# Two cross-attentions of a fused two-layer Perceiver: context loads per batch element, and LayerNorm, copy and output-projection work placed elsewhere

## What is computed

```python
x = x + cross_attention_0(layernorm(x), ctx)   # Wq, Wk, Wv, Wo with biases, 16 heads of 16
x = x + self_attention_0(layernorm(x))
x = x + mixture_of_experts(layernorm(x))       # 8 experts, the best 2 of each token
x = x + cross_attention_1(layernorm(x), ctx)   # one Wq makes q, k and v; Wo; no biases
x = x + causal_rotary_attention_1(layernorm(x))
x = x + ternary_linear(layernorm(x))

def cross_attention(q, ctx):                   # softmax(q k^T / 4) v, then Wo
    ...
```

## Time and profile before

| | |
|---|---|
| median of 3 runs | 2614.49 us |
| the profiled execution: its time, its span | 2609.5 us, 2607.7 us |
| PE, PEld busy | 2407.5 us (92%), 1985.3 us |
| DVE busy | 1836.6 us (70%) |
| ACT busy | 1226.1 us (47%) |
| POOL busy | 838.5 us (32%) |
| moved by DMA | 298.94 MB |
| mean granted TensorE clock | 0.964 |
| x0: first and last scores | 32.8 and 722.9 us |
| x1: first and last scores | 1395.8 and 1971.4 us |

### The profile page before, as it was taken

One profiled execution on the slowest core, in us unless ns is written; L12 is line 12 of the kernel. 1 busy time (PEld: TensorE's weight loads), 2 busy tenths in 40 slices (PEclk: granted clock), 3 DMA queues, 4 the chain that ended last, 5 costly groups with the idle time before them and its releaser, 6 DMA issues. The chain is left out here.

```text
span 2607.7 us, 102881 instructions
## 1 busy us (share of the span) xinstructions
PE 2407.5 (92%) x44640; PEld 1985.3 (76%) x44640; DVE 1836.6 (70%) x3908; ACT 1226.1 (47%) x2728; POOL 838.5 (32%) x732
## 2 busy tenths in 40 slices
PE   7999999999988858999996999998987999999997
PEld 6888888888855546888874777777776888888885
DVE  5777777777766673222226889888986788888886
ACT  4666666666544433332325666666663232332332
POOL 3333333332221112333435344443222233233231
PEclk9999999999998958999998999999998999999998
DMA  6455555554313162111107767778763000000000
GB/s 197 146 152 158 153 155 156 157 157 121 93 53 125 52 239 104 52 48 48 50 30 231 233 192 223 216 224 230 200 195 107 2 3 2 11 11 11 11 11 26
DMA packets 171903, 298.94 MB, mean 115 GB/s; under 512 B 26296, under 2 KB 104252, under 8 KB 161984
## 3 DMA queue, kind: packets, MB, share of 16 engines
q1 hardware_dynamic: 164640, 275.57, 34.9%
q0 software_dynamic: 6816, 16.79, 2.0%
HBM read 170.75 MB, written 78.77 MB: 96 GB/s over the span
## 5 line engine op out<-in xcount | busy, mean ns | idle before, releaser
L801 ACT ACTIVATE prob_x<-ps_score_x,neg_max_x 128x257 f32<-128x257 f32 x1024 | 402.5, 479 | 259.2 <-DVE neg_max_x L853 258.7
L853 DVE TENSOR_REDUCE neg_max_x<-ps_score_x 128x2 f32<-128x514 f32 x512 | 328.8, 683 | 91.7 <-PE ps_score_x L687 91.4
L698 PEld LDWEIGHTS ps_v_x<-v_wide_x,probT_x 128*32 128x32 f32 x18432 | 289.8, 109 | 134.3 <-issue 128.2
L698 PE MATMUL ps_v_x<-v_wide_x,probT_x 128*32 128x68 f32 x18432 | 337.2, 224 | 30.9 <-issue 25.8
L877 DVE STREAM_TRANSPOSE probT_x<-prob_x 128x1152 f32<-128x1152 f32 x256 | 343.9, 1344 | 0.0
L1015 POOL TENSOR_TENSOR ctxT_x_lo<-ready,ctxT_x_hi 128x514 fp32r<-128x514 f32 x128 | 153.2, 1197 | 388.8 <-ACT ctxT_x_hi L780 388.8
L2371 POOL TENSOR_TENSOR rot_s<-turned_s,swapped_s 128x512 f32<-128x512 f32 x128 | 164.4, 1296 | 326.6 <-DVE swapped_s L2300 287.3
L1015 POOL TENSOR_TENSOR split<-loaded,split 128x514 fp32r<-128x514 f32 x128 | 153.0, 1195 | 324.5 <-ACT split L780 324.5
L230 PE MATMUL ps_x<-split,w_q_x_hi 128*128 128x258 f32 x1024 | 209.2, 302 | 22.1 <-POOL split L1015 17.7
L687 PE MATMUL ps_score_x<-kT_x,q_x 32*64 32x257 f32 x4096 | 178.3, 402 | 23.6 <-ACT prob_x L801 18.6
L1911 DVE TENSOR_TENSOR hid_moe<-ps_up_moe,silu_moe 128x512 f32<-128x512 f32 x71 | 49.1, 692 | 203.3 <-PE ps_up_moe L230 203.3
(11 more groups left out here) (290 smaller groups left out, 5997.7 us busy)
## 6 DMA issues: line engine op xcount, KB each, us to landing
v_wide_x<-v_x SPq DMA_DIRECT2D x512, 76.5 KB, 2.3
v_out_x<-v_x SPq DMA_DIRECT2D x128, 306.0 KB, 3.5
v_wide_x<-v_out_x SPq DMA_DIRECT2D x512, 76.5 KB, 2.7
ready<-ctx SPq DMA_DIRECT2D x32, 1028.0 KB, 6.0
loaded<-ctx SPq DMA_DIRECT2D x32, 1028.0 KB, 6.6
gate_whole<-moe_experts SPq DMA_DIRECT2D x32, 256.0 KB, 3.2
lo_out<-gate_whole SPq DMA_DIRECT2D x32, 256.0 KB
w_moe<-lo_out SPq DMA_DIRECT2D x8, 1024.0 KB, 8.8
```

The lines of the kernel that those rows point to most:

```text
L698: ins = pe.do.matmul(self.ps_v[r * T:(r + 1) * T, b % 2, :, :], self.probT[b % 3][:, r, n * T:(n + 1) * T], self.v_wide[b % 4][:, :, r, n, ...
L801: act.do.activation(self.prob[b % 3][:, r, 0:S], self.ps[:, r, 0:S], ACT.Exp, bias=self.neg_max[b % 2][:, r:r + 1]).then_inc(*s.exp.at(tag ...
L853: dve.do.tensor_reduce(self.neg_max[b % 2][:, r], self.ps[:, r, 0:S], AX_X, ALU.max, negate=True).then_inc(*s.neg_max.at(tag, b, half))
```

## The change

In both cross-attentions:

- The context is loaded per batch element, 257 KB at a time, one load in every turn, from a DRAM array and into an SBUF buffer in which each element is contiguous. Four semaphores (one for each place in a group) replace two. A load of element `i + 7` stands in turn `i`, behind waits for the split of element `i - 1` and for the landing of element `i + 3`.

In x1 alone (`self.opening`):

- `take_stats` of the next group stands in turn 12 of the group before (turn 4 for group 1), `root` in 13 (5); scaling is two pieces of two row blocks in turns 6 and 7 on ACT (`scale_on_act`), with one more POOL multiplication (`shift`) and one more DVE one (`minus_mean`).
- `keep_attn` is on ACT, in front of the exponentials.
- `project_out` stands behind `weigh_v` and in front of `project_k`; `add_out` at the end of the same turn on DVE, no longer at the beginning of the next.
- `load_y` issues its three loads in turns 3, 4 and 5.
- The first statistics of `s1` stand in turn 4 of the last group.

In x0 alone: statistics a turn sooner (4 and 5), root in 5, scaling in 6. `bq` and `m_zero` become events of other semaphores.

```diff
-        on_act = [t for t in tags if t in ("s0", "moe")]
+        on_act = [t for t in tags if t in ("s0", "moe", "x1")]
...
-        self.pad, self.bq = count("pad", cross()), count("bq", [()])
-        self.ctx_in = [count(f"ctx_in{i}", cross(g[i::2]), 16) for i in range(2)]
+        self.pad = count("pad", [("x0",), ("bq",), ("x1",)])
+        self.ctx_in = [count(f"ctx_in{i}", cross(b[i::BPG]), 16) for i in range(BPG)]
...
-    def scale_on_act(self, act, i):
+    def scale_on_act(self, act, i, some=range(GPS)):
         c, tag = self.c, self.tag
         act.wait_ge(c.shift, tag, i)
         if i >= len(self.xn):
             act.wait_ge(c.T, tag, i - len(self.xn), KD - 1)
-        for j in range(GPS):
+        for j in some:
             ins = act.do.activation(self.rows(i)[:, j, :], self.X[:, GPS * i + j, :], ACT.Identity, bias=self.shift[:, j:j + 1],
                                     scale=self.rstd[:, j:j + 1])
-        ins.then_inc(*c.xn.at(tag, i))
+        if some[-1] == GPS - 1:
+            ins.then_inc(*c.xn.at(tag, i))
...
-        self.ctx_in = [loaded[:, i * ctx:(i + 1) * ctx].rearrange("p (k b s) -> p k b s", k=KD, b=BPG) for i in range(2)]
+        self.ctx_in = [loaded[:, i * ctx:(i + 1) * ctx].rearrange("p (b k s) -> p b k s", k=KD, b=BPG) for i in range(2)]
...
-        self.ln = LayerNorm(nc, stack, s, tag, X, consts, self.xT)
+        self.ln = LayerNorm(nc, stack, s, tag, X, consts, self.xT, on_act=bool(opening))
...
-        def load_ctx(g):
-            if g >= 2:
-                sp.wait_ge(s.ctx_hi, tag, (g - 1) * BPG - 1)
-                sp.wait_ge(s.ctx_lo, tag, (g - 1) * BPG - 1)
-            sp.do.dma_start(self.ctx_in[g % 2][:, :, :, :], self.ctx[g]).then_inc(*s.ctx_in[g % 2].at(tag, g))
+        def load_ctx(b):
+            if b >= 2 * BPG:
+                sp.wait_ge(s.ctx_hi, tag, b - 2 * BPG)
+                sp.wait_ge(s.ctx_lo, tag, b - 2 * BPG)
+            if b >= BPG:
+                sp.wait_ge(s.ctx_in[b % BPG], tag, b - BPG)
+            sp.do.dma_start(self.ctx_in[b // BPG % 2][:, b % BPG, :, :], self.ctx[b // BPG][:, b % BPG, :, :]).then_inc(
+                *s.ctx_in[b % BPG].at(tag, b))
...
-        def load_y(i):
+        def load_y(i, some=("x", 0, 1)):
...
+            for n in some:
+                if n == "x":
+                    continue
...
-        load_ctx(0)
+        for b in range(BPG):
+            load_ctx(b)
...
-            if self.opening and i % BPS == 4 and i // BPS + 2 < SG:
-                load_y(i // BPS + 2)
-            if i % BPG == 1 and (i + 7) // BPG < G:
-                load_ctx((i + 7) // BPG)
+            if self.opening and i % BPS in (3, 4, 5) and i // BPS + 2 < SG:
+                load_y(i // BPS + 2, [("x", 0, 1)[i % BPS - 3]])
+            if i and i + 2 * BPG - 1 < B:
+                load_ctx(i + 2 * BPG - 1)
...
+            a, rest = divmod(i - self.lag - 9, BPS // 2)
+            if not rest and a >= 0 and self.opening:
+                project_out(a)
...
-            a, rest = divmod(i - self.lag - 9, BPS // 2)
-            if not rest and a >= 0:
+            if not rest and a >= 0 and not self.opening:
...
+        def keep_attn(p):
+            a, k = p // 4, p % 4
+            act.wait_ge(s.weighed_T, tag, p)
+            if a >= 2:
+                act.wait_ge(s.o_ps, tag, a - 2)
+            act.do.activation(self.attn[a % 2][:, :, k, :], banks["weighed", p][:, 0:P].rearrange("p (r q) -> p r q", q=T),
+                              ACT.Copy).then_inc(*s.attn.at(tag, p))
...
+        if self.opening:
+            self.ln.scale_on_act(act, 0)
...
+            p, odd = divmod(i - self.lag - 3, 2)
+            if self.opening and not odd and 0 <= p < B // 2:
+                keep_attn(p)
...
+            if self.opening and n < SG and j in (6, 7):
+                self.ln.scale_on_act(act, n, range(2 * (j - 6), 2 * (j - 6) + 2))
...
+            if self.opening and not rest and a >= 0:
+                add_out(2 * a)
+                add_out(2 * a + 1)
+            if self.opening and (i == 4 or j == 12 and n + 1 < SG):
+                ahead = 1 if i == 4 else n + 1
+                dve.wait_ge(s.y_added, ahead)
+                for group in range(GPS):
+                    self.ln.take_stats(dve, ahead, group)
...
-                if j in (5, 6):
-                    dve.wait_ge(s.x_out, tag, GPS - 1)
-                    for half in range(GPS // 2):
-                        self.opening.ln.take_stats(dve, 0, (j - 5) * (GPS // 2) + half)
+                if j == 4:
+                    for group in range(GPS):
+                        self.opening.ln.take_stats(dve, 0, group)
...
-            if n < SG and j in (5, 6):
+            if not self.opening and n < SG and j in (4, 5):
                 dve.wait_ge(s.x_in[1], SG - 1)
-                if self.opening:
-                    dve.wait_ge(s.y_added, n)
                 for half in range(GPS // 2):
-                    self.ln.take_stats(dve, n, (j - 5) * (GPS // 2) + half)
-            if n < SG and j == 7:
+                    self.ln.take_stats(dve, n, (j - 4) * (GPS // 2) + half)
+            if not self.opening and n < SG and j == 6:
...
-            if n < SG and j == 6:
+            if not self.opening and n < SG and j == 5:
                 self.ln.root(pool, n)
+            if self.opening and (i == 5 or j == 13 and n + 1 < SG):
+                self.ln.root(pool, 1 if i == 5 else n + 1)
...
-        "ctx": i["ctx_1024"].transpose(0, 2, 1).reshape(G, BPG, KD, P, S).transpose(0, 3, 2, 1, 4),
+        "ctx": i["ctx_1024"].transpose(0, 2, 1).reshape(G, BPG, KD, P, S).transpose(0, 3, 1, 2, 4),
```

40 lines of the change are left out of this document (22 added, 18 removed).

## The result

The changed kernel takes 2589.31 us, the median of 4 runs (2583.66 to 2593.48); the kernel before takes 2613.64 beside it (2611.96 to 2615.35). The ratio is 0.9905, with a 95% interval of 0.9885 to 0.9926: 24 us faster. The forecast was 38 us faster, 2576.5. The sign and the range held; of the 38 us a good third did not come. In another session the changed kernel took 2589.33 us against 2611.1, ratio 0.9913 (0.9886 to 0.9940).

What follows compares the result with a forecast made beforehand. PE was taken to bound x0; x1 was tight on PE and DVE, with 51.6 us of PE idle. Terms summing to -38 took the profiled 2609.5 us to 2571.5, hence a median of 2576.5; 8-in-10 range 2556 to 2604.

Steps and rivals of the forecast that it cites:

- Level loads: x1: smaller context loads and spaced load_y free PE's instruction fetches, taking 21 of 23.8 us of waits without a releaser.
- Rival A: x1: fetches aren't freed, load size being irrelevant or the queues full altogether; 2607 us, partly up to 2590; chance 0.17.
- Clock: x1: PE's lower clock around idle turns costs 11 us of full speed; 8 us gained, between 0 and 11.
- LayerNorm: x1: scaling and copy moved from DVE to ACT take 12 us out of PE's waits, 3 put back for ACT.
- Rival B: x1: ACT becomes late in DVE's place in each group's turns 6 to 9; 2594 us, chance 0.15.
- V's DMA waits: x1: PE's waiting for V's DMA loses 1.5 of 2.5 us.
- The ring of three banks: x1: with project_out before K, K's second half waits for add_out to free a bank; +1 us, between 0 and 7.
- Statistics of group 1 in turn 4: x1: the statistics put into that turn, which has only project_out, cost 1 us at most.
- x1's beginning: Start of x1: first scaling on ACT behind the last K copy, plus a POOL step; 1.4 us later, between 0 and 2.5.
- x0, statistics a turn sooner: x0: moving LayerNorm's statistics one turn earlier changes nothing, 0 us.
- x0's start: Start of x0: three further SP issues delay the constants by 0 us, at the end of the range by 1.4.
- Rival C: x1: context pieces before V's way out make V's DRAM trip set the pace; slower, 2624 us, chance 0.07.

Runs made afterwards that it cites:

- second execution: The changed kernel, unaltered, run and traced again in a later job: 22.7 us below the kernel before, x1 in 544.5 us.
- without the context: The changed kernel with x1 loading the context of its first 8 elements only and reusing it: x1 531.6 us, fetch stalls 2.9 us.
- level loads alone: The kernel before with only the per-element 257 KB context loads in both cross-attentions: 3.7 us faster by the ratio, x1 571.9 us.
- changed kernel with group loads: The changed kernel with a group's context in one 1028 KB load again, at the old places: 3.9 us below the kernel before.
- pieces together: The changed kernel with a group's four 257 KB context loads issued together every fourth turn: fetch stalls 14.4 us, waits for V 26.3 us.

## Why the prediction was right in sign and too large in size

*Level loads: the term that failed.* I took 21 of 23.8 us; 6.8 went by the same rows (23.8 to 17.0), 9 by gaps (26.0 to 17.0), 14.6 in the second execution. The 23.8 left out a row of the same view, so it was 25.9 to 17.0 there as well:

```profile
PE ps_score_x L687 <- issue: 2.1, 2, 1.2
```

That context loads hold the fetches was right: without them 2.9 us are left. Wrong was how: that a fetch "starts only when the load is through", and from it "if the hold lasts as long as the load, 5.9 us becomes about 1.5". In the trace of before, 12 of the 17 packets that end a stall begin while a load of 512 KB or more is still in flight, 8 of them with 1.8 to 8.7 us of it to go; the packet of the earlier trace rows, 0.3 us ahead of the load's landing, is one of four that come near an end. And a piece of a quarter lands in 4.2 us, in a queue that carries the same bytes. Rival A (0.17) was this half: the queues are full altogether, share 0.80 over x1 now, part of the stalls stays, and its sign, more than 15 us of waits for "issue", is met by 17.0. Its price, 2607, was too high, and "with fewer of them kept, up to 2590" is where the result lies.

Of the two rules of the Trainium skill that stood against my reading, "DMA: Bandwidth & Descriptors", on queues, rings and completion order, lets an engine change queues at packet boundaries. The trace agrees with it in the 12 of 17 packets that begin within a load; that no stall would come of the loads, as I had concluded from it, is refuted by the 2.9 us without the context. "Runtime: NRT & Kernel Launch", on instruction fetch mechanics, gives PE a buffer of 2048 instructions, which packets at most 506 records apart wouldn't let run empty; the stalls that came and went with the context traffic don't fit that.

*Clock: -8 predicted.* The clock records of x1, between first and last scores, show 20.5 us at the lower level before and 6.8 after. Half of such a stretch is lost: 6.8 us gained. Right in size, though the level loads alone had the same 6.8 us with all their stalls. But up to 3.4 us were lost again at x1's start, and some 3 behind x0: in 728.6 to 732.0 and 735.5 to 738.9 us the changed kernel has the lower level where before had the higher. These two rows are before's and after's first stretch:

```profile
728.60:732.00 3.40, 1.54 (x69) 1.01 (x57) 0.69 (x4) 0.00 (x0) 0.00 (x0) 1.00 0.00 0
```

```profile
728.60:732.00 3.40, 3.40 (x16) 2.58 (x16) 0.00 (x0) 0.00 (x0) 0.00 (x0) 0.51 0.02 5
```

The change edits nothing in that stretch. In every other trace, the level loads alone and the changed kernel with group loads among them, the records show 3.4 to 10.2 us of the lower level there, within 21 us of x0's last scores; the one trace of before is the odd one. So part of the 8 us between the stages may be before's good luck and no cost of the change.

*LayerNorm, -12 + 3 = -9 predicted:* the rest of the idle time fell by 13.6 us. Right, and half as much again: ACT's lateness, priced at 3, is hardly seen. Four scalings cost ACT 606 ns each, `keep_attn` 278 ns, against my 0.39 us and 0.3 us. Rival B (0.15) did not come: scores wait 7.5 us for exponentials, not 12 or more.

*V's DMA waits, -1.5:* -1.0, and +1.0 in the second execution. *The ring of three banks, +1 between 0 and 7:* 2.7, in 12 waits of at most 0.2 us. *Statistics of group 1 in turn 4, 1 us at most:* turn 5 of the first group has a wait of 1.5 us behind them, 2.1 without the context. *`keep_attn`:* I argued with DVE's missing air, and the run with it back on DVE shows that it gave nothing.

*x1's beginning, +1.4 between 0 and 2.5: missed.* Four scalings on ACT start behind K's last copy and take 2.06 us, PE waits 2.43 and then runs at half clock. From x0's last to x1's first scores the five kernels with DVE's first scaling take 672.9 to 675.5 us, the nine with ACT's 676.4 to 683.3, 5.5 us more on average (the stretch behind x0 is in it). In the two profiled executions PE's first K projection of x1 starts 12.3 us ahead of the first scores before and 16.2 after: 1.8 more for the wait (2.43 against 0.60) and 2.0 more from the transposes to the scores, at the lower clock. I priced the scaling and forgot what an idle PE does to the clock.

*x0, statistics a turn sooner: 0 predicted.* It costs 3.7 us: 687.8 or 687.9 us in three kernels with the old turns, 691.4 to 692.2 in those with the new. Turn 7 of a group went from 4.91 to 5.8 us. PE's waits of 60 to 700 us in the changed kernel name it:

```profile
PE ps_x L230 <- DVE v_x L896: 5.1, 7, 1.0
```

Before, the same view has:

```profile
PE ps_x L230 <- DVE v_x L869: 0.6, 2, 0.3
```

The scaling now stands in front of DVE's turning of V in a turn in which PE has no slack for it. I had written that nothing which *relieves* an engine could help x0, and did not ask what moving its work could cost. That before's profiled x0 had 1.6 us of stalls of its own hid part of it (+1.7).

*x0's start: 0 predicted, -5.0 found*, partly chance (29.6 us with group loads, 26.5 to 30.7 with level ones). *Rival C* did not come: `v_out` lands in 4.2 us against 4.8 from which it would cost, and V's waits are 1.5 and 3.5 us. Its mechanism is real, as the pieces together show.

In all: -25.1 us in x1 where the terms said -38.5 (measured one by one they give -27.8: fetch -9.0, clock -6.8, LayerNorm -13.6, V -1.0, ring +2.6; 2.7 us are not accounted for); +8.0 between the stages where I had 1.4; -3.4 in x0 and its start where I had -0.9. Of the signs named for being right, waits for "issue" under 6 us (17.0) and x1 in about 538 us (550.6) failed; turns 7 and 8 near 4 us (3.6 to 4.9 in the seven groups), the clock and x0 within 2 us came.

What stays open: how a fetch is held in a queue of small loads, since neither the size of one load (level loads alone kept 25.4 us) nor, it seems, the queue's depth (the pieces together stall no more than the changed kernel) decides it; what sets the time at the lower clock in x1; and the clock behind x0. A variant with the two `s_qkv` loads a turn apart, against the stall of turn 114, was not run.

## What to carry to other kernels

Two kinds of stall in the same turns shade each other, so a part that shows little alone can be worth more beside the other; try both together before dropping either, and split the surplus by kind of wait, since here the shading was only a third of it. A load cut into four doesn't land four times as soon when the queue is near full (6.5 us became 4.2): read the landing of a small DMA in the same stretch, and use that. Where PE sets the pace, ask of every moved instruction what now stands behind it on its own engine. Keep the clock as a row of its own beside the idle time: 2.4 us of waiting at x1's start had 6.8 us of the lower level behind it, while all of x1 with level loads alone, 56 us idle, had no more than that.
